# Recurrence of a delta-rule attention block: column sums moved to TensorE, two matrices in turns on VectorE, GpSimd left out

## The chip, the cores and the metric

The kernel runs on one core of one Trainium2 chip. The metric is the time of one execution of the whole program on the device, in microseconds (us). Before the change three runs gave a median of 5632.02 us (5631.69 to 5635.43).

## The reference, cut to what matters

The program is two transformer layers in float32 on an input of 2 x 2048 tokens with 128 features. The changed part is the first sublayer of layer 0, a chunked attention with a matrix memory M (8 x 8 for each of 16 heads) that every token updates:

```python
k = k / jnp.maximum(jnp.linalg.norm(k, axis=-1, keepdims=True), 1e-12)
alpha = jax.nn.sigmoid(alpha_raw) * 0.5
beta = jax.nn.sigmoid(beta_raw) * 2.0
def t_step(M, kv):
    k_t, v_t = kv
    Mk = jnp.einsum('bhde,bhe->bhd', M, k_t)
    forget = Mk[..., :, None] * k_t[..., None, :]
    write = v_t[..., :, None] * k_t[..., None, :]
    return (M - alpha * forget + beta * write, None)
```

M is updated token by token over 64-token chunks, each chunk reads M as it stood at its start, and the rest of the sublayer is a softmax attention inside the chunk. The kernel cuts the 4096 tokens into 128 pieces of 32 tokens, one to a partition. The effect of a piece on M is an affine map: M becomes M A + B. So a recurrence of 32 steps, run for all 128 pieces at once, works out A (the decay rows, starting from the identity) and B (the write rows, starting from zero) for every head. A later, short scan puts the 128 maps together.

## The kernel before, in words

`two_layer_kernel` runs its stages one after another; an all-engine barrier stands between them. The change lies in the first of the three blocks of `delta_attention_stage`, which the lines below number as the profile does.

**Ahead of the recurrence.** SyncE (SP) loads inputs. VectorE (DVE) normalises the input groups; TensorE (PE) transposes them (L243) into `hT`, ScalarE (ACT) copies them out of PSUM (L268), and PE makes q, k, v of each of the 32 positions with one matmul each (L250), which ACT copies to `qs`, `ks`, `vs` (L271 to L273). `hT` isn't read again in this stage. DVE normalises `ks` (L323 to L329), multiplies `vs` by beta in 32 instructions (L337), sets `state` to zero and its decay rows to the identity (L339, L340), and lets GpSimd (POOL) go.

**The recurrence.** `state` is [128 pieces, 16 heads, 16 rows, 8 columns]: rows 0 to 7 of a head are A, rows 8 to 15 are B. A step multiplies the state by the key (L347), sums over the 8 columns (L348), multiplies by alpha, which carries its minus sign (L349), adds the value to the write rows (L350), multiplies that vector by the key (L351) and adds the product to the state (L352). DVE does this for heads 0 to 11 in a hardware loop of 32 turns; each instruction waits for the one before it. POOL does the same for heads 12 to 15 in a loop of its own (L290 to L300), with the key copied first and the column sums made by three halving additions (L294 to L296). The two engines don't wait for each other inside the loops. PE and ACT have nothing to do.

**Behind it.** DVE waits for POOL (L354), lays the state out anew in two copies (L355, L356) and releases PE (L357), which makes 16 transposes in four groups (L258); ACT copies each group out (L277). That ends the block. The next block is the scan over the 128 pieces (L376 on POOL, L388 on PE, L413 on DVE), then come the chunk attention and all other stages, none of which the change touches. SP stores q, k and v to DRAM in the same block (L228 to L235) and isn't waited for inside it, but for the DVE's wait for the first two stores ahead of L337.

`Steps` gives each instruction of an engine a semaphore increment and, unless `settle=False`, makes the engine wait for it. `wait(eng, sem, value)` is a wait that falls away for values of zero and below.

Of the kernel before, what the change touches and what calls it, by code (L numbers as in the profile page):

```python
# [13 lines left out]
ALU = mybir.AluOpType  # L14
AX = mybir.AxisListType
# [41 lines left out]
def wait(eng, sem, value):  # L57

    if not isinstance(value, int) or value > 0:
        eng.wait_ge(sem, value)  # L60
# [103 lines left out]
def delta_attention_stage(nc, x_dram, xr, mods, w_qkvT, w_oT, alpha_raw, beta_raw, tables, qkv_dram):  # L164

    H, DH, SUB, N_SUB = 16, 8, 32, 128
    with ExitStack() as ctx:
        sem = ctx.enter_context(stage_semaphores(nc, "da"))
        keep = lambda n, shape, dt=F32: ctx.enter_context(nc.sbuf_tensor(f"da_{n}", shape, dt))  # L170
        mem = keep("mem", [128, 64, 128])
        ident = keep("ident", [128, 128])
# [5 lines left out]
        with ExitStack() as c2:  # L178
            sb = lambda n, shape, dt=F32: c2.enter_context(nc.sbuf_tensor(f"da_{n}", shape, dt))
            ps = [c2.enter_context(nc.psum_tensor(f"da_psa{i}", [128, 512], F32)) for i in range(8)]  # L180
            hT = sb("hT", [128, 4096])
            st, mv = sb("st", [128, 4, 6]), sb("mv", [128, 4, 2])
            mean, var, rstd, half, tmp = (sb(n, [128, 32]) for n in ("mean", "var", "rstd", "half", "tmp"))
            h = sb("h", [128, 2, 4, 128])
# [4 lines left out]
            state = sb("state", [128, H, 16, DH])  # L189
            prod = sb("prod", [128, H, 16, DH])  # L190
            dots = sb("dots", [128, H, 16])

            flat_state = prod[:, :, :, :].rearrange("p a b c -> p a (b c)")
# [6 lines left out]
            state_init, pool_state_done, pool_seq, ones_set = sem("state_init"), sem("pool_state_done"), sem("pool_seq"), sem("ones_set")  # L200

            H_DVE = 12
            key = sb("key", [128, DH * (H - H_DVE)])

            def recurrence_operands(t, hs):

                k_t = ks[:, ds(t, 1), :].rearrange("p o (h e) -> p (o h) e", e=DH)[:, hs, :]
                v_t = vs[:, ds(t, 1), hs, 0:DH].rearrange("p o h e -> p (o h) e")
                n = hs.stop - hs.start
                kb = k_t.rearrange("p h (o e) -> p h o e", o=1).to_broadcast([128, n, 16, DH])  # L210
                ub = dots[:, hs, :].rearrange("p h (r o) -> p h r o", o=1).to_broadcast([128, n, 16, DH])
                return kb, ub, v_t, alpha[:, hs].rearrange("p (h o) -> p h o", o=1).to_broadcast([128, n, 16])

            with nc.Block() as block:
# [22 lines left out]
                def _(pe):  # L237
# [13 lines left out]

                    pe.wait_ge(state_done, 1)
                    pe.wait_ge(v_out, SUB)
                    for j in range(4):
                        wait(pe, tr_done, 2 * (j - 1))
                        for i in range(4):
                            n = 4 * j + i
                            last = nc.tensor.transpose(ps[j % 2][:, 128 * i:128 * i + 128], flat_state[:, n, :], ident[:, :])  # L258
                        last.then_inc(tr_ps, 1)
# [19 lines left out]
                @block.gpsimd  # L279
                def _(pool):  # L280
                    step = Steps(pool, pool_seq)

                    nc.gpsimd.memset(vs[:, :, :, DH:DH + 1], 1.0).then_inc(ones_set, 1)
                    pool.wait_ge(state_init, 1)
                    hs = slice(H_DVE, H)
                    with pool.Fori(0, SUB) as t:
                        step.turn(0, t, 9)
                        _, ub, v_t, alpha_b = recurrence_operands(t, hs)
                        k_t = ks[:, ds(t, 1), DH * H_DVE:DH * H].rearrange("p o d -> p (o d)")
                        step(nc.gpsimd.tensor_copy(key[:, :], k_t))  # L290
                        kb = key[:, :].rearrange("p (h o e) -> p h o e", o=1, e=DH).to_broadcast([128, H - H_DVE, 16, DH])
                        step(nc.gpsimd.tensor_tensor(prod[:, hs, :, :], state[:, hs, :, :], kb, ALU.mult))

                        step(nc.gpsimd.tensor_tensor(prod[:, hs, :, 0:4], prod[:, hs, :, 0:4], prod[:, hs, :, 4:8], ALU.add))  # L294
                        step(nc.gpsimd.tensor_tensor(prod[:, hs, :, 0:2], prod[:, hs, :, 0:2], prod[:, hs, :, 2:4], ALU.add))
                        step(nc.gpsimd.tensor_tensor(dots[:, hs, :], prod[:, hs, :, 0], prod[:, hs, :, 1], ALU.add))  # L296
                        step(nc.gpsimd.tensor_tensor(dots[:, hs, :], dots[:, hs, :], alpha_b, ALU.mult))
                        step(nc.gpsimd.tensor_tensor(dots[:, hs, DH:16], dots[:, hs, DH:16], v_t, ALU.add))
                        step(nc.gpsimd.tensor_tensor(prod[:, hs, :, :], ub, kb, ALU.mult))
                        step(nc.gpsimd.tensor_tensor(state[:, hs, :, :], state[:, hs, :, :], prod[:, hs, :, :], ALU.add))  # L300
                    pool.sem_inc(pool_state_done, 1)

                @block.vector
                def _(dve):
# [14 lines left out]
                    flat = prod[:, :, :, :].rearrange("p a b c -> p (a b c)")  # L319
# [14 lines left out]
                    for t in range(0, SUB, 8):  # L334
                        for i in range(8):
                            vi = vs[:, t + i, :, 0:DH]
                            step(nc.vector.tensor_tensor(vi, vi, beta[:, :].rearrange("p (h o) -> p h o", o=1).to_broadcast([128, H, DH]), ALU.mult), settle=(i == 7))  # L337

                    step(nc.vector.memset(state[:, :, :, :], 0.0))  # L339
                    step(nc.vector.memset(state[:, :, :, :].rearrange("p h r e -> p h (r e)")[:, :, 0:64:9], 1.0))  # L340
                    dve.sem_inc(state_init, 1)
                    before = step.base + step.n
                    hs = slice(0, H_DVE)
                    with dve.Fori(0, SUB) as t:
                        step.turn(before, t, 6)
                        kb, ub, v_t, alpha_b = recurrence_operands(t, hs)
                        step(nc.vector.tensor_tensor(prod[:, hs, :, :], state[:, hs, :, :], kb, ALU.mult))  # L347
                        step(nc.vector.tensor_reduce(dots[:, hs, :], prod[:, hs, :, :], AX.X, ALU.add))  # L348
                        step(nc.vector.tensor_tensor(dots[:, hs, :], dots[:, hs, :], alpha_b, ALU.mult))  # L349
                        step(nc.vector.tensor_tensor(dots[:, hs, DH:16], dots[:, hs, DH:16], v_t, ALU.add))  # L350
                        step(nc.vector.tensor_tensor(prod[:, hs, :, :], ub, kb, ALU.mult))  # L351
                        step(nc.vector.tensor_tensor(state[:, hs, :, :], state[:, hs, :, :], prod[:, hs, :, :], ALU.add))  # L352
                    step.turn(before, SUB, 6)
                    dve.wait_ge(pool_state_done, 1)  # L354
                    step(nc.vector.tensor_copy(flat_state[:, 0:DH, :].rearrange("p e (h r) -> p h r e", r=DH), state[:, :, 0:DH, :]))  # L355
                    step(nc.vector.tensor_copy(flat_state[:, DH:16, :].rearrange("p d (h e) -> p h d e", e=DH), state[:, :, DH:16, :]))  # L356
# [1868 lines left out]
```

## Time and profile before

| what | value |
|---|---|
| median of 3 runs | 5632.02 us |
| time of the profiled execution | 5640.35 us |
| span of its trace, first to last instruction | 5638.6 us |
| granted TensorE clock, mean | 0.901 |
| busy: PE, DVE, ACT, POOL | 82%, 72%, 56%, 53% |
| the recurrence (L347 to L357) | about 142 to 493 us of the span |

### The profile page before, as it was taken

Reading aid. Unit: us, or ns where it says so; the run is one execution under the profiler, and the core shown is the slowest. Engines: PE = TensorE matmul, PEld = TensorE weight load, DVE = VectorE, ACT = ScalarE, POOL = GpSimd, SP = SyncE. Lnnn points to the kernel's source line nnn. Section 1 sums busy time; section 2 is a strip of 40 time slices with the busy share of each in tenths; the row PEclk is TensorE's granted clock in tenths of the full one; section 3 lists DMA queues with packets and bytes.
Section 4 is the critical chain, followed back from the end, with each engine's and each line's share of the span. In section 5 each row is a group of like instructions: output and inputs, shape, how many; then the busy total and the mean of one; then the engine's idle time right before and its main releaser. Section 6 shows DMA issues by size and latency. Waiting matters only on the chain. (4 is left out here: it accounts for less than half of the span.)

```text
span 5638.6 us, 215664 instructions
## 1 busy us (share of the span) xinstructions
PE 4650.3 (82%) x78080; PEld 3324.1 (59%) x78080; DVE 4062.7 (72%) x8694; ACT 3158.8 (56%) x6668; POOL 2979.6 (53%) x4109
## 2 busy tenths in 40 slices
PE   2004776999999999999999999999992874998997
PEld 2003653666666666667666767676762553666665
DVE  5995557777777777777777777777775446776675
ACT  1000443677677767766676767676761122676675
POOL 0887104666666666666666666666650001555552
PEclk6555887999999999999999999999996567999998
DMA  1000114454545454545454555554540002443342
GB/s 69 0 0 0 35 31 118 123 140 128 138 127 138 126 141 128 138 131 138 131 134 131 136 134 131 135 133 134 131 119 15 0 0 61 114 112 109 107 113 77
DMA packets 708750, 564.88 MB, mean 100 GB/s; under 512 B 227460, under 2 KB 633704, under 8 KB 707848
## 3 DMA queue, kind: packets, MB, share of 16 engines
q1 hardware_dynamic: 694920, 538.05, 36.3%
q10 hardware_dynamic: 13312, 22.02, 1.2%
q14 instruction: 449, 3.68, 0.2%
q8 instruction: 69, 1.13, 0.1%
HBM read 360.07 MB, written 200.02 MB: 99 GB/s over the span
## 5 line engine op out<-in xcount | busy, mean ns | idle before, releaser
L2080 POOL TENSOR_TENSOR L_qk<-L_cos_part,L_sin_part 128x512 f32<-128x512 f32 x896 | 1128.9, 1274 | 165.0 <-DVE L_sin_part L1965 164.6
L1750 ACT ACTIVATE L_squares<-L_ps_q 128x512 f32<-128x512 f32 x896 | 535.0, 597 | 981.1 <-PE L_ps_q L1502 975.0
L1502 PE MATMUL L_ps_q<-L_w_qkv,L_xT 128*128 128x512 f32 x1792 | 971.8, 625 | 27.8 <-DVE L_sin_part L1965 10.2
L2071 POOL TENSOR_TENSOR L_qk<-L_qk,L_rnorm 128x1024 f32<-128x1024 f32 (+1 forms) x512 | 864.7, 1689 | 20.3 <-POOL L_rnorm L2061 0.5
L1537 PEld LDWEIGHTS L_ps_t<-L_ident,L_qk 128*128 128x128 f32 x3584 | 446.4, 141 | 474.6 <-issue 376.4
L1964 DVE TENSOR_TENSOR L_cos_part<-L_ps_q,L_rot 128x512 f32<-128x512 f32 x896 | 610.3, 681 | 43.0 <-POOL L_rot L2090 35.1
L1965 DVE TENSOR_TENSOR L_sin_part<-L_ps_q,L_rot 128x512 f32<-128x512 f32 x896 | 610.1, 681 | 0.0
L1966 DVE TENSOR_REDUCE L_sumsq<-L_squares 128x8 f32<-128x512 f32 x896 | 605.7, 676 | 0.0
L2055 POOL TENSOR_TENSOR L_nw_a<-L_rnorm 128x32 f32<-128x32 f32 (+1 forms) x256 | 60.0, 234 | 1026.6 <-ACT L_rnorm L1780 1026.5
L1537 PE MATMUL L_ps_t<-L_ident,L_qk 128*128 128x128 f32 x3584 | 539.4, 273 | 2.5 <-POOL L_qk L2071 1.9
L1761 ACT ACTIVATE L_qkT<-L_ps_t 128x512 f32<-128x512 f32 x896 | 530.0, 591 | 13.9 <-PE L_ps_t L1537 13.5
L1589 PEld LDWEIGHTS L_ps_t<-L_ident,L_probs 128*128 128x128 f32 x2048 | 215.2, 141 | 413.7 <-issue 350.1
L2090 POOL TENSOR_TENSOR L_rot<-L_rot_base,L_qk_scales 128x256 f32<-128x256 f32 x256 | 187.3, 732 | 506.6 <-DMA L_qk_scales<-in_L_ffn_k_scale 500.3
L1603 PE MATMUL L_ps_q<-L_w_out,L_outT 128*128 128x128 f32 x3584 | 445.8, 276 | 2.8 <-ACT L_outT L1769 1.7
L1603 PEld LDWEIGHTS L_ps_q<-L_w_out,L_outT 128*128 128x128 f32 x3584 | 422.1, 193 | 5.1 <-issue 4.4
L1634 PE MATMUL L_ps_s<-L_qkT 64*32 64x64 f32 (+1 forms) x26624 | 415.1, 228 | 0.2 <-ACT L_qkT L1761 0.2
L1930 DVE RECIPROCAL L_p_rec<-L_ps_o 128x8 f32<-128x8 f32 (+1 forms) x512 | 103.0, 201 | 408.2 <-PE L_ps_o L1655 302.6
L1574 PE MATMUL L_ps_t<-L_w_qkv,L_xT 128*128 128x512 f32 x768 | 393.7, 594 | 0.6 <-issue 0.6
L1949 DVE TENSOR_TENSOR L_probs<-L_ps_s,L_neg_max 128x512 f32<-128x512 f32 x512 | 354.4, 692 | 53.2
L1589 PE MATMUL L_ps_t<-L_ident,L_probs 128*128 128x128 f32 x2048 | 327.5, 283 | 75.1 <-issue 62.8
L1634 PEld LDWEIGHTS L_ps_s<-L_qkT 64*32 64x32 f32 (+1 forms) x26624 | 322.0, 107 | 108.2 <-issue 108.2
L1935 DVE TENSOR_TENSOR L_att<-L_ps_o,L_p_rec 128x512 f32<-128x512 f32 (+1 forms) x512 | 320.2, 625 | 53.2
(295 smaller groups left out, 9429.7 us busy)
## 6 DMA issues: line engine op xcount, KB each, us to landing
L_val<-v_rows SPq DMA_DIRECT2D x896, 260.0 KB, 3.9
v_rows<-L_val SPq DMA_DIRECT2D x384, 260.0 KB, 2.1
v_rows<-L_val SPq DMA_DIRECT2D x512, 65.0 KB, 2.0
L_rot_base<-in_rot SPq DMA_DIRECT2D x256, 128.0 KB, 2.1
v_rows<-L_val SPq DMA_DIRECT2D x128, 130.0 KB, 2.1
L_x_in<-x_rows SPq DMA_DIRECT2D x512, 32.0 KB, 1.7
mid_rows<-z SPq DMA_DIRECT2D x256, 64.0 KB, 1.6
L_f_in<-mid_rows SPq DMA_DIRECT2D x256, 64.0 KB, 2.0
```

What stands on the lines that cost most here:

```text
L1502: nc.tensor.matmul(ps_q[j % 2][:, :], xT[:, parity(t), :], w_qkv[:, 0:2, 256 * j:256 * j + 256], start=True, stop=True).then_inc(S["proj_p ...
L1537: last = nc.tensor.transpose(ps_t[0][:, 128 * i:128 * i + 128], qk[:, parity(t), h, s, 128 * i:128 * i + 128], ident[:, :])
L1589: last = nc.tensor.transpose(ps_t[2 - NS][:, 128 * i:128 * i + 128], probs[:, h, 128 * i:128 * i + 128], ident[:, :])
L1603: last = nc.tensor.matmul(ps_q[0][:, 0:128], outT[:, u, :], w_out[:, u, :], start=(u == 0), stop=(u == U - 1))
L1634: last = nc.tensor.matmul(S_VIEW[W * a:W * a + W, p, i, :], qkT[rows, 0, u, W + W * a:2 * W + W * a], qkT[rows, kk, u, W * a:W * a + 2 * W ...
L1750: nc.scalar.activation(squares[:, j % 2, :], ps_q[j % 2][:, :], ACT.Square).then_inc(S["sq_done"], 1)
L1761: nc.scalar.activation(dst, ps_t[0][:, :].rearrange("x (a u q) -> x a u q", a=2, u=2), ACT.Copy).then_inc(S["qkT_done"], 1)
L1964: nc.vector.tensor_tensor(R4(cos_part[:, j % 2, :]), qkp, cs[:, :, 0, :, :, :].to_broadcast([128, 2, 4, 2, 32]), ALU.mult)
L1965: nc.vector.tensor_tensor(R4(sin_part[:, j % 2, :]), qkp[:, :, :, ::-1, :], cs[:, :, 1, :, :, :].to_broadcast([128, 2, 4, 2, 32]), ALU.mul ...
L1966: nc.vector.tensor_reduce(sumsq[:, t % 2, j, :], squares[:, j % 2, :].rearrange("x (g d) -> x g d", g=8), AX.X, ALU.add).then_inc(S["ss_do ...
L2071: nc.gpsimd.tensor_tensor(v, v, r, ALU.mult).then_inc(S["normed"], 1)
L2080: nc.gpsimd.tensor_tensor(qk[:, t % 2, h, s, :], cos_part[:, j % 2, :], sin_part[:, j % 2, :], ALU.add).then_inc(S["added"], 1)
```

## The change

`state` and `prod` become [128, 2, 8, 128]: part 0 is A (decay), part 1 is B (write); within a part the column comes first, then head and row. Each part has 1024 elements in a partition, all on DVE.

A step for one part is now: DVE multiplies the part by the key times alpha (`k_forget`, made once beforehand for all steps, in the memory of `hT`); PE adds the eight columns of the product with eight matmuls against the identity into one PSUM bank (and for part 1 adds the value, times beta, with a ninth); DVE multiplies that sum, read from PSUM, by the key; DVE adds the product to the part. DVE takes the two parts in turns. Both loops, DVE's and PE's, are written out over the 32 steps. POOL's loop is gone; POOL only writes the ones column of `vs`, as before. The products with beta and with alpha are one instruction each. The identity is set by eight small memsets. At the end one copy lays part 1 out anew; part 0 is transposed as it stands.

```diff
-            state = sb("state", [128, H, 16, DH])
-            prod = sb("prod", [128, H, 16, DH])
-            dots = sb("dots", [128, H, 16])
+            state = sb("state", [128, 2, DH, 128])
+            prod = sb("prod", [128, 2, DH, 128])
...
+            k_forget = hT[:, :].rearrange("p (t d) -> p t d", t=SUB)
+            def over_rows(k):
+                return k.rearrange("p (h e o) -> p e h o", e=DH, o=1).to_broadcast([128, DH, H, DH])
+            def blocks(a):
+                return a.rearrange("p e (h r) -> p e h r", r=DH)
...
                 # TensorE
+                    for t in range(SUB):
+                        for part in range(2):
+                            pe.wait_ge(multiplied[part], t + 1)
+                            for e in range(DH):
+                                last = nc.tensor.matmul(ps[2 + part][:, 0:128], ident[:, :], prod[:, part, e, :], start=(e == 0), stop=(part == 0 and e == DH - 1))
+                            if part == 1:
+                                last = nc.tensor.matmul(ps[3][:, 0:128].rearrange("p (h d) -> p h d", d=DH), ident[:, :], vs[:, t, :, 0:DH], start=False, stop=True)
+                            last.then_inc(summed[part], 1)
...
-                            last = nc.tensor.transpose(ps[j % 2][:, 128 * i:128 * i + 128], flat_state[:, n, :], ident[:, :])
+                            last = nc.tensor.transpose(ps[j % 2][:, 128 * i:128 * i + 128], (state[:, 0, n, :] if n < DH else prod[:, 1, n - DH, :]), ident[:, :])
                 # GpSimd: the whole loop of L287 to L301 goes
...
                 # VectorE
-                    for t in range(0, SUB, 8):
-                        for i in range(8):
-                            vi = vs[:, t + i, :, 0:DH]
-                            step(nc.vector.tensor_tensor(vi, vi, beta[:, :].rearrange("p (h o) -> p h o", o=1).to_broadcast([128, H, DH]), ALU.mult), settle=(i == 7))
+                    vb = vs[:, :, :, 0:DH]
+                    per_head = lambda a: a[:, :].rearrange("p (o h u) -> p o h u", o=1, u=1).to_broadcast([128, SUB, H, DH])
+                    nc.vector.tensor_tensor(vb, vb, per_head(beta), ALU.mult).then_inc(factors, 1)
+                    nc.vector.tensor_tensor(k_forget.rearrange("p t (h e) -> p t h e", e=DH), ks[:, :, :].rearrange("p t (h e) -> p t h e", e=DH), per_head(alpha), ALU.mult).then_inc(factors, 1)
                     step(nc.vector.memset(state[:, :, :, :], 0.0))
...
+                    for e in range(DH):
+                        nc.vector.memset(blocks(state[:, 0, :, :])[:, e, :, e], 1.0).then_inc(state_init, 1)
+                    dve.wait_ge(state_init, DH)
+                    dve.wait_ge(factors, 2)
+                    def multiply(part, t):
+                        wait(dve, updated[part], t)
+                        nc.vector.tensor_tensor(blocks(prod[:, part, :, :]), blocks(state[:, part, :, :]), over_rows(k_forget[:, t, :]), ALU.mult).then_inc(multiplied[part], 1)
+                    def update(part, t):
+                        dve.wait_ge(summed[part], t + 1)
+                        u = ps[2 + part][:, 0:128].rearrange("p (o h r) -> p o h r", o=1, r=DH).to_broadcast([128, DH, H, DH])
+                        nc.vector.tensor_tensor(blocks(prod[:, part, :, :]), u, over_rows(ks[:, t, :]), ALU.mult).then_inc(outer[part], 1)
+                        dve.wait_ge(outer[part], t + 1)
+                        nc.vector.tensor_tensor(state[:, part, :, :], state[:, part, :, :], prod[:, part, :, :], ALU.add).then_inc(updated[part], 1)
+                    multiply(0, 0)
+                    for t in range(SUB):
+                        multiply(1, t)
+                        update(0, t)
+                        if t + 1 < SUB:
+                            multiply(0, t + 1)
+                        update(1, t)
+                    for part in range(2):
+                        dve.wait_ge(updated[part], SUB)
+                    step(nc.vector.tensor_copy(prod[:, 1, :, :].rearrange("p d (h e) -> p e h d", e=DH), blocks(state[:, 1, :, :])))
                     dve.sem_inc(state_done, 1)
```

## Rows read from the trace of the kernel before

**Rows 1.** The chain of waits from 132 to 500 us: who waited, us in total, times, longest

```profile
PE da_psa L258 <- DVEq L357: 383.5, 1, 383.5
...
DVE da_prod L347 <- DVE da_state L352: 13.1, 31, 0.5
...
DVE da_prod L355 <- POOLq L301: 6.6, 1, 6.6
```

**Rows 2.** Busy time by stretch: length, PE, PEld, DVE, ACT, POOL, clock, DMA

```profile
142.00:491.00 349.00, 0.00 (x0) 0.00 (x0) 320.52 (x192) 0.00 (x0) 312.53 (x288) 0.50 0.00 0
```

**Rows 3.** Timeline of one late recurrence step: start us, duration us, engine, line, operation

```profile
463.33 2.60 DVE L347 TENSOR_TENSOR da_prod<-da_state,da_ks 128x1536 f32<-128x1536 f32 x1 [0.42 <-DVE da_state L352]
...
465.97 1.75 DVE L348 TENSOR_REDUCE da_dots<-da_prod 128x192 f32<-128x1536 f32 x1
...
469.53 2.65 POOL L300 TENSOR_TENSOR da_state<-da_state,da_prod 128x512 f32<-128x512 f32 x1
471.10 2.70 DVE L352 TENSOR_TENSOR da_state<-da_state,da_prod 128x1536 f32<-128x1536 f32 x1
...
474.22 2.60 DVE L347 TENSOR_TENSOR da_prod<-da_state,da_ks 128x1536 f32<-128x1536 f32 x1 [0.42 <-DVE da_state L352]
```

**Rows 4.** Timeline of DVE around the recurrence's start, 126 to 152 us

```profile
127.65 4.43 DVE L329 TENSOR_TENSOR da_ks<-da_ks,da_rk 128x4096 f32<-128x4096 f32 x1
132.11 6.93 DVE L337 TENSOR_TENSOR da_vs<-da_vs,da_beta 128x128 f32<-128x128 f32 x32
139.53 1.76 DVE L339 MEMSET da_state<- 128x2048 f32 x1 [0.49 <-DVE da_vs L337]
141.49 0.17 DVE L340 MEMSET da_state<- 128x128 f32 x1 [0.19 <-DVE da_state L339]
142.01 1.79 DVE L347 TENSOR_TENSOR da_prod<-da_state,da_ks 128x1536 f32<-128x1536 f32 x1 [0.36 <-DVE da_state L340]
143.84 1.75 DVE L348 TENSOR_REDUCE da_dots<-da_prod 128x192 f32<-128x1536 f32 x1
```

**Rows 5.** Timeline of DVE at 1942 us: PSUM inputs, no wait for the instruction before

```profile
1941.62 0.68 DVE L1964 TENSOR_TENSOR L_cos_part<-L_ps_q,L_rot 128x512 f32<-128x512 f32 x1
1942.21 0.68 DVE L1965 TENSOR_TENSOR L_sin_part<-L_ps_q,L_rot 128x512 f32<-128x512 f32 x1
```

**Rows 6.** Timeline of DVE at 67 us: L103 waits for L102 just before it

```profile
67.79 0.69 DVE L102 TENSOR_TENSOR da_h<-da_h,mods 128x512 f32<-128x512 f32 x1
68.52 0.69 DVE L103 TENSOR_TENSOR da_h<-da_h,mods 128x512 f32<-128x512 f32 x1
```

**Rows 7.** Timeline of PE: the group of transposes released by that L103

```profile
69.27 1.12 PE L243 MATMUL da_psa<-da_ident,da_h 128*128 128x128 f32 x4 [1.30 <-DVE da_h L103]
```

**Rows 8.** Timeline of PEld, one record for each half of a 384-column matmul

```profile
88.04 0.34 PEld L250 LDWEIGHTS da_psa<-da_w,da_hT 128*128 128x128 f32 x1 [0.30 <-issue]
88.68 0.34 PEld L250 LDWEIGHTS da_psa<-da_w,da_hT 128*128 128x128 f32 x1 [0.30 <-issue]
```

**Rows 9.** Timeline of PE at 937 us: eight 128-column float32 matmuls

```profile
937.64 1.95 PE L1603 MATMUL L_ps_q<-L_w_out,L_outT 128*128 128x128 f32 x16
```

**Rows 10.** Busy time of PE by stretch: length, busy (records), granted clock, DMA

```profile
66.00:85.00 19.00, 8.63 (x32) 0.50 0.00 0
86.00:92.00 6.00, 6.00 (x10) 0.50 0.00 0
92.00:109.00 17.00, 17.00 (x54) 1.00 0.01 1
...
580.00:590.00 10.00, 7.00 (x43) 0.99 0.01 2
590.00:600.00 10.00, 4.74 (x21) 0.52 0.19 51
600.00:610.00 10.00, 7.05 (x224) 0.97 0.24 59
```

**Rows 11.** Timeline around the recurrence's end: DVE, PE, ACT

```profile
491.26 1.26 DVE L355 COPY da_prod<-da_state 128x1024 f32<-128x1024 f32 x1 [6.59 <-POOLq L301]
492.56 0.69 DVE L356 COPY da_prod<-da_state 128x1024 f32<-128x1024 f32 x1
...
493.36 3.84 PE L258 MATMUL da_psa<-da_ident,da_prod 128*128 128x128 f32 x16 [383.52 <-DVEq L357]
494.58 0.60 ACT L277 ACTIVATE da_trans_a<-da_psa 128x512 f32<-128x512 f32 x1 [384.09 <-PE da_psa L258]
...
497.30 0.60 ACT L277 ACTIVATE da_trans_b<-da_psa 128x512 f32<-128x512 f32 x1 [0.26 <-PE da_psa L258]
```

**Rows 12.** Timeline of PE at 957 us: a train that stops with nothing to wait for

```profile
957.29 0.39 PE L1655 MATMUL L_ps_o<-L_val,L_probsT 64*32 64x65 f32 x18 [1.48 <-issue]
```

More of the change, by code:

```diff
@@ L188, in delta_attention_stage @@
             vs = sb("vs", [128, SUB, H, DH + 1])
-            state = sb("state", [128, H, 16, DH])
-            prod = sb("prod", [128, H, 16, DH])
-            dots = sb("dots", [128, H, 16])
-            flat_state = prod[:, :, :, :].rearrange("p a b c -> p a (b c)")
+            state = sb("state", [128, 2, DH, 128])
+            prod = sb("prod", [128, 2, DH, 128])
             rk, rk_half, rk_tmp, rk_x = (sb(n, [128, SUB * H]) for n in ("rk", "rk_half", "rk_tmp", "rk_x"))
@@ L198, in delta_attention_stage @@
             k_normed, stored, state_done, tr_ps, tr_done = (sem(n) for n in ("k_normed", "stored", "state_done", "tr_ps", "tr_done"))
[L200 to L212, printed above, removed]
+            ones_set = sem("ones_set")
+            state_init, factors = sem("state_init"), sem("factors")
+            multiplied, summed, outer, updated = ([sem(f"{n}_{part}") for part in ("decay", "write")] for n in ("multiplied", "summed", "outer", "updated"))
+            k_forget = hT[:, :].rearrange("p (t d) -> p t d", t=SUB)
[3 more added lines that the diff above has]
+                return a.rearrange("p e (h r) -> p e h r", r=DH)
             with nc.Block() as block:
@@ L280, in _ @@
                 def _(pool):
-                    step = Steps(pool, pool_seq)
                     nc.gpsimd.memset(vs[:, :, :, DH:DH + 1], 1.0).then_inc(ones_set, 1)
[L284 to L301, printed above, removed]
                 @block.vector
@@ L318, in _ @@
                     dve.wait_ge(k_out, SUB)
-                    flat = prod[:, :, :, :].rearrange("p a b c -> p (a b c)")
+                    flat = prod[:, :, :, :].rearrange("p a e x -> p (a e x)")
                     kf = ks[:, :, :].rearrange("p t d -> p (t d)")
@@ L339, in _ @@
+                    nc.vector.tensor_tensor(vb, vb, per_head(beta), ALU.mult).then_inc(factors, 1)
+                    nc.vector.tensor_tensor(k_forget.rearrange("p t (h e) -> p t h e", e=DH), ks[:, :, :].rearrange("p t (h e) -> p t h e", e=DH), per_head(alpha), ALU.mult).then_inc(factors, 1)
                     step(nc.vector.memset(state[:, :, :, :], 0.0))
-                    step(nc.vector.memset(state[:, :, :, :].rearrange("p h r e -> p h (r e)")[:, :, 0:64:9], 1.0))
-                    dve.sem_inc(state_init, 1)
@@ L342, in _ @@
[L342 to L356, printed above, removed]
+                    for e in range(DH):
+                        nc.vector.memset(blocks(state[:, 0, :, :])[:, e, :, e], 1.0).then_inc(state_init, 1)
```

## The prediction

> **What bounds the kernel now.** I began with the granted clock and the waits. The chain that ended last shows only the final stage, so I took the waits of the stretch of the change: PE sits 383.5 us for DVE's release behind the recurrence, and nothing else waits there for long [rows 1]. Stages stand between barriers, so every microsecond by which that release comes earlier shortens the program. The busy times by stretch say who works: of 349 us DVE is busy 320.5, POOL 312.5, PE and ACT not at all, with the clock at half [rows 2]. Neither loop waits for the other by a semaphore, yet both are slow. The timeline shows how: a turn takes 10.89 us (463.33 to 474.22), and in it the same 1536-element instruction that took 1.79 us in the first turn takes 2.60, and the state's addition 2.70 [rows 3, 4]. The instruction that runs with one SBUF input, the sum over columns, takes 1.75 both times. So the bound is DVE and POOL together: their instructions hold each other up. POOL ends last, by 6.6 us [rows 1].
>
> **The change part by part.** *Cost of a DVE instruction.* New ones have 1024 elements. Durations at 512, 1536 and 4096 elements are 0.69, 1.76 to 1.79 and 4.43 us [rows 4, 6]; they lie on a line of 1.042 us per 1000 elements plus 0.16, which gives 1.23 us at 1024. A PSUM input doesn't make it dearer: 0.68 at 512 [rows 5]. Start to start it depends on the wait: an instruction that waits for the one before follows after 0.73 us at 512 (0.533 us of elements and 0.19), one that doesn't after 0.59 to 0.60 (0.533 and 0.065) [rows 5, 6]. At 1024 these are 1.26 and 1.13 us.
>
> *DVE's step.* Six instructions for each t. The first product waits for the part's addition just before it, the addition waits for the outer product just before it: four pitches of 1.26. Each outer product follows a product that it doesn't depend on: two of 1.13. Together 7.30 us, and 32 x 7.30 = 233.6 us. With POOL idle I take the undisturbed durations. POOL's nine instructions a turn, alpha's and the value's additions (L349, L350) and the loop's 0.42 us [rows 3] are gone.
>
> *PE's step.* 17 matmuls of 128 columns, 34 records. At 2.4 GHz sixteen records take 1.95 us, their last one's tail included, some 0.112 each [rows 9]. At 1.2 GHz a record of 384 columns takes 0.64 us start to start, so 0.213 for 128 [rows 8]. Handing over costs 0.06 us from DVE to PE (68.52 + 0.69 to 69.27 [rows 6, 7]) and 0.1 from PE's end (493.36 + 1.12) to the reader [rows 7, 11]. Eight sums are then ready 0.06 + 1.95 + 0.1 = 2.1 us after the product at full clock, nine after 2.3; at half clock 0.06 + 16 x 0.213 + 0.2 of tail + 0.1 = 3.8 and 4.2. Between a product's end and the moment DVE wants its sum lie the other part's outer product and addition and one more product: 1.13 - 0.10 + 2 x 1.26 = 3.55 us. So at full clock PE hides with 1.2 us to spare. Without that cover, at half clock, 0.2 and 0.65 us of each step show: 8.15 us a step.
>
> *Start.* At the first sum there is only one product to hide behind (3.8 - 1.1 = 2.6 us at half clock), and I give a step or so to the clock's rise: 3.6 us. Recurrence: 237.2.
>
> *Ahead of it.* The 32 small instructions (6.93 us) go; two of 4096 elements come at 4.43 each, the second overlapped: 8.8. The memset stays at 1.76, and eight tiny ones take the place of one; each costs between 0.07 and 0.17 (L340 [rows 4]), I take 0.8 in all. The loop's entry (0.36 [rows 4]) goes. From 132.11 the first product starts at about 143.8 instead of 142.0: 1.8 lost. SP's three stores run beside this and nobody new waits for them; POOL's and SP's queues get nothing.
>
> *Behind it.* The last addition ends at 143.8 + 237.2 = 381.0. One copy with a strided output stays, at L355's 1.26, not L356's 0.69 [rows 11], and 0.2 for its waits; PE's transposes start at 382.6 against 493.36: 110.8 won. PE comes to them warm: four take some 0.7 instead of 1.12, and ACT's four copies become the bound; about 1.1 won of the 4.5 from 493.36 to the last copy's end [rows 11]. The scan behind begins with POOL, so a warm PE wins it nothing that I count.
>
> **Sum.** 5640.35 (the profiled execution; its span is 5638.6) - 111.9 = 5528.4. The median is 8.3 us below that execution, so the prediction for the median is 5632.0 - 111.9 = **5520**.
>
> **A page against the rows.** The pitch depends on the semaphore wait: 0.73 us with one on the instruction before, 0.60 without [rows 5, 6]. The Trainium skill (VectorE: DVE Perf Modes, The DRAIN you can't avoid) says that the next instruction starts only when the pipe is empty and that "the semaphore costs nothing extra here". The trace doesn't agree; by that rule all six pitches would be alike.
>
> **The rivals.**
> *All pitches alike.* If waits cost nothing, a step is 6 x 1.13 = 6.8 us and the time 5504; if there is never an overlap, 6 x 1.26 = 7.56 and 5528. Rows 5 and 6 speak against both, though neither pair has this kernel's operands. The first is the page's rule above. 0.04 and 0.08; the second stays within my range.
>
> *The clock stays or falls back to 1.2 GHz.* PE would then need 7.25 us of 8.15 a step. For: PE busy in bursts for 8.63 of 19 us left it at half, and it fell after a stretch with 4.74 of 10 busy. Against: six us of uninterrupted matmuls raised it, and it stayed up with 7.0 of 10 busy [rows 10]. Here records fill (2.0 + 2.2) / 7.3 = 0.57 of the time at full clock, between those two, but 0.9 at half clock, so it is raised whenever it falls. At half clock throughout: 32 x 8.15 = 261, time 5546; alternating, between. The Trainium skill (TensorE: Matmul & The Clock Gate, A second HAM failure mode: psum-queue depth-cycling) tells of a kernel that cycled PSUM banks with short idles and saw the clock oscillate; no row here shows that for this pattern. 0.12.
>
> *Weight loads aren't hidden (slower).* Each record brings a load of the identity. At half clock such a load is recorded with 0.34 us [rows 8], more than the 0.213 that the columns take. If loads ran in series with 128-column records, the step would be at least 34 x 0.34 = 11.6 us, 32 x 11.6 = 370, and the time 5520 + (370 - 237) = 5653, slower. It decides from a record pitch of about 0.31 us on, where a step reaches (237.2 + 111.9) / 32 = 10.9 us, what it is today. Against: at full clock sixteen records with their loads take 1.95 us [rows 9], and four transposes at half clock 1.12 [rows 7], so loads overlap. 0.02.
>
> *Instruction supply.* 1088 matmuls and some 190 DVE instructions are written out, no loop. A train of PE stopped once for 1.48 us with nothing to wait for [rows 12]. On PE 1.2 us of each is hidden; on DVE none is. A dozen stops on both would cost 5 to 15 us. 0.06.
>
> *It does nothing.* That POOL isn't what slows DVE, and 1024 elements cost as much as in rows 3 (1.45 times): step 10.6, time about 5626. Rows 4 exclude it nearly. 0.01.
>
> **How the numbers follow.** The forecast case has 0.67 and gives 5520 with 5 us to either side for setup, handovers and shifted later stages. The range reaches from there over part of the first rival to the cold clock and a few supply stops: 5510 to 5550. No change can be told from noise within 0.2% (11 us). Faster takes all cases but the serial loads and part of the last: 0.97, same 0.01, slower 0.02.
>
> **What would show it.** The six DVE instructions at 1.22 to 1.23 us, none near 1.7; pitches 1.26, 1.13, 1.26 in turn; a step of 7.3; the wait of DVE for PE near zero but at the first sum; PE's records 0.112 apart and the clock at 1.0 from some 10 us into the recurrence; PE released at about 383 us; the scan behind unchanged in length. I am wrong if DVE waits for PE each step, if the clock stands at 0.5 there, if pitches are alike, or if stages behind the block change by more than 3 us.

## The result, and the profile after

The changed kernel takes 5504.03 us (median of four runs, 5502.36 to 5505.12) against 5633.73 us for the kernel before on the same chip: a ratio of 0.9771 with a 95% interval of 0.9759 to 0.9783, 129.7 us less. The forecast was 5520 with a range of 5510 to 5550. The sign and the mechanism were right; the time came out 6 us below the range. One rival of the prediction has this very time, 5504 for pitches that are all alike; the pitches below speak against it. One run of the kernel before, beside e9 to e11, was slow at 8020.41 us, and the ratios leave it out.

The span is 5502.0 us, and the profiled execution took 5503.74. From the page, busy times with counts, then the granted clock in 40 slices:

```profile
PE 4777.1 (87%) x79168; PEld 3443.6 (63%) x79168; DVE 3958.7 (72%) x8670; ACT 3156.6 (57%) x6668; POOL 2667.5 (48%) x3821
...
PEclk6987979999999999999999999999995567999998
```

PE has 1088 records more, the 34 a step of the 32 steps. To see where time went, I took each stage's length from its first to its last instruction. The block with the recurrence shrank from 461.9 us (36.0 to 497.9) to 349.0 (34.7 to 383.7): 112.9 us, where the prediction's sum has 111.9. So the missing part isn't in the recurrence. The rest of the program, whose code is the same, became shorter by 136.6 - 112.9 = 23.7 us in the two profiled executions, and by 129.7 - 112.9 = 16.8 if the medians are taken: the profiled execution of before lies 7 us above its median.

The recurrence in the timeline of the kernel after, one full step (start us, duration us, engine, line, operation):

```profile
150.28 1.22 DVE L341 TENSOR_TENSOR da_prod<-da_psa,da_ks 128x1024 f32<-128x1024 f32 x1
...
150.42 2.05 PE L254 MATMUL da_psa<-da_prod,da_ident 128*128 128x128 f32 x16 [1.32 <-DVE da_prod L335]
151.53 1.23 DVE L343 TENSOR_TENSOR da_state<-da_state,da_prod 128x1024 f32<-128x1024 f32 x1
152.79 1.22 DVE L335 TENSOR_TENSOR da_prod<-da_state,da_hT 128x1024 f32<-128x1024 f32 x1
153.94 1.22 DVE L341 TENSOR_TENSOR da_prod<-da_psa,da_ks 128x1024 f32<-128x1024 f32 x1
...
155.18 1.23 DVE L343 TENSOR_TENSOR da_state<-da_state,da_prod 128x1024 f32<-128x1024 f32 x1
...
156.44 1.23 DVE L335 TENSOR_TENSOR da_prod<-da_state,da_hT 128x1024 f32<-128x1024 f32 x1
157.59 1.22 DVE L341 TENSOR_TENSOR da_prod<-da_psa,da_ks 128x1024 f32<-128x1024 f32 x1
```

Read the start times: 150.28, 151.53, 152.79, 153.94, 155.18, 156.44, 157.59. The pitches are 1.25, 1.26 and 1.15 in turn and a step is 7.31 us; [rows 3] had 10.89. An outer product, which waits for nothing that DVE has just done, starts 0.07 us before the product ahead of it ends. Sixteen records of PE take 2.05 us and lie wholly beside DVE.

The chain of waits from 142 to 380 us has for DVE one line, the first sum:

```profile
DVE da_prod L341 <- PE da_psa L254: 2.7, 1, 2.7
```

The busy time of PE by stretch in the kernel after (length, busy by records, granted clock, DMA) shows the rise and fall of the clock, and the timeline the end of the block:

```profile
142.00:147.50 5.50, 4.70 (x22) 0.50 0.00 0
147.50:160.00 12.50, 7.98 (x64) 1.00 0.01 1
376.00:379.60 3.60, 0.23 (x2) 1.00 0.00 0
379.60:383.00 3.40, 3.40 (x16) 0.50 0.00 0
```

```profile
378.17 1.09 DVE L354 COPY da_prod<-da_state 128x1024 f32<-128x1024 f32 x1
...
379.37 1.78 PE L265 MATMUL da_psa<-da_ident,da_state 128*128 128x128 f32 x8 [3.83 <-DVEq L355]
...
383.11 0.60 ACT L284 ACTIVATE da_trans_b<-da_psa 128x512 f32<-128x512 f32 x1 [0.26 <-PE da_psa L265]
```

The clock is at 2.4 GHz from 147.5 us on, 5 us after the first sum began, and the whole recurrence keeps it (PE is busy for 0.60 of the time from 143 to 371 us by its records). After 3.8 us without a matmul it is at 1.2 GHz again from 379.6 us on, just behind the transposes' start, so they take from 379.37 to 383.71, 4.3 us, against 4.5 before [rows 11].

### The profile page after: what moved, and what is told of

Its sections match the earlier page's. It is cut to its first block and busy times, and to the rows that moved or that the text cites. A ratio compares the mean times of both kernels' runs of the same rounds, so it can differ in the third digit from the quotient of the medians.

```text
span 5502.0 us, 216728 instructions
## 1 busy us (share of the span) xinstructions
PE 4777.1 (87%) x79168; PEld 3443.6 (63%) x79168; DVE 3958.7 (72%) x8670; ACT 3156.6 (57%) x6668; POOL 2667.5 (48%) x3821
## 3 DMA queue, kind: packets, MB, share of 16 engines
q8 instruction: 77, 1.26, 0.1%
## 5 line engine op out<-in xcount | busy, mean ns | idle before, releaser
L1500 PE MATMUL L_ps_q<-L_w_qkv,L_xT 128*128 128x512 f32 x1792 | 969.4, 623 | 23.7 <-DVE L_sin_part L1963 11.0
```

What stands on the lines that cost most here:

```text
L1500: nc.tensor.matmul(ps_q[j % 2][:, :], xT[:, parity(t), :], w_qkv[:, 0:2, 256 * j:256 * j + 256], start=True, stop=True).then_inc(S["proj_p ...
```

## The experiments

Medians of before stand beside each experiment's own, from the same chip. "Block" is the length of the stage with the recurrence, "first" and "second" are the two local-block stages behind it; all three from the profiled execution, one for each kernel.

| kernel | block | first | second | median |
|---|---|---|---|---|
| before | 461.9 | 3402.9 | 881.1 | 5633.7 |
| after | 349.0 | 3389.8 | 874.4 | 5504.0 |
| e3 before, no POOL loop | 377.9 | 3401.3 | 881.2 | 5554.1 |
| e7 before, all heads on DVE | 450.6 | 3401.2 | 881.2 | 5625.2 |
| e8 after, POOL busy | 436.4 | 3389.9 | 874.3 | 5592.2 |
| e4 after, no turns | 600.1 | 3392.5 | 873.1 | 5758.2 |
| e1 before, PE code | 461.4 | 3398.0 | 881.2 | 5629.1 |
| e2 after, PE shift | 349.1 | 3396.9 | 873.8 | 5510.5 |
| e5 before, DVE code | 461.2 | 3396.8 | 877.3 | 5623.6 |
| e6 after, 64 on DVE | 349.0 | 3413.8 | 873.8 | 5530.1 |
| e11 after, 128 on DVE | 349.1 | 3390.7 | 869.9 | 5505.5 |
| e12 before, both codes | 461.8 | 3398.6 | 874.5 | 5625.4 |
| e9 trim | 342.8 | 3397.0 | 873.9 | 5507.3 |
| e10 trim, warm | 342.1 | 3389.9 | 873.0 | 5502.4 |

**Is it contention? e3: POOL's loop taken out of the kernel before, and heads 12 to 15 with it.**

```diff
-                    pool.wait_ge(state_init, 1)
...
-                        step(nc.gpsimd.tensor_tensor(state[:, hs, :, :], state[:, hs, :, :], prod[:, hs, :, :], ALU.add))
```

> The kernel before without POOL's loop: heads 12 to 15 are left out, VectorE's 12 heads stay. Theory (VectorE and POOL hold each other up): VectorE's 1536-element products fall from 2.5 to 1.76 us, a step from 10.9 to 8.5, the block by 77 + 6.6 us, the time to about 5550. Rival (the instructions are slow for their operands, and POOL only ends late): a step stays above 10 us and only the 6.6 us of waiting go, 5627.

Measured: 5554.06 us against 5633.59, a ratio of 0.986 (0.9845 to 0.9876); the block 377.9 us, 84.0 less. Its timeline:

```profile
198.62 1.76 DVE L330 TENSOR_TENSOR da_prod<-da_state,da_ks 128x1536 f32<-128x1536 f32 x1 [0.42 <-DVE da_state L335]
...
204.79 1.76 DVE L335 TENSOR_TENSOR da_state<-da_state,da_prod 128x1536 f32<-128x1536 f32 x1
206.97 1.76 DVE L330 TENSOR_TENSOR da_prod<-da_state,da_ks 128x1536 f32<-128x1536 f32 x1 [0.42 <-DVE da_state L335]
```

The products and the addition fell to 1.76 us from the 2.60 and 2.70 of [rows 3] and a turn to 8.35. The two loops did hold each other up, with no semaphore between them.

**What is that worth by itself? e7: all 16 heads on DVE, as before otherwise.**

```diff
-                    hs = slice(0, H_DVE)
+                    hs = slice(0, H)
```

(and POOL's loop out, as in e3)

> The recurrence as before, but all 16 heads on VectorE and none on POOL: no PE sums, no contention. A step of 12 heads took 8.35 us with POOL's loop taken out; 512 more elements in four instructions (2.13) and a tenth for the small ones make 10.6, so the block is about 449 us and the time 5625. That would show that leaving POOL idle by itself is worth some 10 us, and that PE's sums are worth the other 100. Rival (POOL alone is the trouble and VectorE has room): a step below 9 us and a time near 5560.

Measured: 5625.17 us against 5633.51, ratio 0.9984 (0.9975 to 0.9994); the block 450.6 us, the 2048-element instructions 2.29 us each. So POOL's quarter of the work had cost DVE more than it saved: with all heads on DVE the block is 11 us shorter. The other 101.6 us of the change's 112.9 are the rest of the change. What they consist of can be read from e7's timeline:

```profile
199.26 2.29 DVE L334 TENSOR_TENSOR da_prod<-da_dots,da_ks 128x2048 f32<-128x2048 f32 x1
...
206.62 2.29 DVE L331 TENSOR_REDUCE da_dots<-da_prod 128x256 f32<-128x2048 f32 x1
208.94 0.42 DVE L332 TENSOR_TENSOR da_dots<-da_dots,da_alpha 128x256 f32<-128x256 f32 x1
209.51 0.29 DVE L333 TENSOR_TENSOR da_dots<-da_dots,da_vs 128x128 f32<-128x128 f32 x1
209.84 2.29 DVE L334 TENSOR_TENSOR da_prod<-da_dots,da_ks 128x2048 f32<-128x2048 f32 x1
```

A step takes 10.58 us. The column sum and the two small instructions, which the change takes off DVE, have 3.22 us of it (206.62 to 209.84), 103 us in 32 steps. The other 7.36 us, three instructions of 2048 elements and the loop's turn, are about what the six of 1024 elements take in the kernel after (7.31).

**The same contention, made in the new kernel. e8: POOL at work beside it.**

```diff
+                    pool.wait_ge(factors, 2)
+                    with pool.Fori(0, 150) as t:
+                        step.turn(1, t, 1)
+                        step(nc.gpsimd.tensor_tensor(junk[:, 0, :], junk[:, 1, :], junk[:, 2, :], ALU.mult))
```

> The changed kernel with POOL multiplying 512-element tiles of its own in SBUF 150 times beside the recurrence. Theory (instructions of VectorE with two SBUF inputs and instructions of POOL exclude each other): L335 and L343 rise from 1.22 to between 1.8 and 2.5 us, the outer product L341, which has one input in PSUM, keeps 1.22, the step rises from 7.3 to 10 or more while POOL works, the time to 5560 to 5600. Rival (only POOL's work on the same tiles did harm): a step of 7.3 and a time of 5504.

Measured: 5592.18 us against 5633.51 (0.9929, 0.9914 to 0.9944), 88 us above the changed kernel; the block takes 436.4 us, 87.4 more. From its timeline, a stretch of the recurrence and the end of the block:

```profile
198.80 1.22 DVE L351 TENSOR_TENSOR da_state<-da_state,da_prod 128x1024 f32<-128x1024 f32 x1
199.21 1.93 POOL L296 TENSOR_TENSOR da_junk<-da_junk 128x512 f32<-128x512 f32 x1 [0.45 <-POOL da_junk L296]
...
200.06 2.17 DVE L343 TENSOR_TENSOR da_prod<-da_state,da_hT 128x1024 f32<-128x1024 f32 x1
...
202.16 1.21 DVE L349 TENSOR_TENSOR da_prod<-da_psa,da_ks 128x1024 f32<-128x1024 f32 x1
...
209.27 2.17 DVE L343 TENSOR_TENSOR da_prod<-da_state,da_hT 128x1024 f32<-128x1024 f32 x1
...
443.14 0.60 ACT L286 ACTIVATE da_trans_b<-da_psa 128x512 f32<-128x512 f32 x1 [0.26 <-PE da_psa L267]
...
469.65 1.26 POOL L296 TENSOR_TENSOR da_junk<-da_junk 128x512 f32<-128x512 f32 x1 [0.45 <-POOL da_junk L296]
```

Not all of the 88 us are contention. A step takes 9.2 us (200.06 to 209.27) instead of 7.31, less than the 10 that I expected, and 32 of them make 60 us. The block's work is done at 443.74; then the barrier waits 27 us for the rest of POOL's 150 instructions, which take 1.26 us each when DVE is idle.

POOL's instruction starts during the addition (L351), is recorded with 1.93 us and ends at 201.14; the product (L343), begun meanwhile, is recorded with 2.17 and ends 1.09 us after POOL's, little less than its usual time. The tiles have nothing in common, so it isn't the data. My expectation was half right: I had the addition slower too, but it keeps 1.22 to 1.23 us in all 64 records. POOL is the one that is late there, since the two engines fall into step. The outer product, which has one input in PSUM, keeps 1.21. The Trainium skill (SBUF — State Buffer, SBUF: two separate sides) calls the port pair that VectorE and GpSimd share an exclusive lock, which a VectorE instruction with two SBUF inputs needs and the loser waits for; the trace agrees with both halves of it, 2.17 us with two SBUF inputs and 1.21 with one.

**Does the cover matter? e4: the parts one after another.**

```diff
-                        multiply(1, t)
-                        update(0, t)
...
+                        for part in range(2):
+                            multiply(part, t)
+                            update(part, t)
```

> The changed kernel with the parts one after another on VectorE (product, sum, outer product, addition of one part, then of the other), so that nothing covers PE's sums. If the clock stays at 2.4 GHz a step is 1.23 + 2.1 + 1.26 + 1.13 and the same with 2.3, 11.7 us, and the time 5504 + 32 x 4.4 = 5644. If it falls to 1.2 GHz, the sums take 3.8 and 4.2 us, a step is 15.2 and the time about 5757. PE would be busy for 0.36 of the time at full clock, which I expect to be too little to hold it: above 5700.

Measured: 5758.18 us against 5633.59, ratio 1.0221 (1.0205 to 1.0236), slower than before the change. The first fence is its timeline, the second its busy time of PE by stretch:

```profile
303.19 3.78 PE L254 MATMUL da_psa<-da_prod,da_ident 128*128 128x128 f32 x16 [3.71 <-DVE da_prod L335]
...
307.44 1.22 DVE L341 TENSOR_TENSOR da_prod<-da_psa,da_ks 128x1024 f32<-128x1024 f32 x1 [4.30 <-PE da_psa L256]
```

```profile
300.00:620.00 320.00, 164.19 (x714) 0.62 0.00 0
```

The same 16 records take 3.78 us instead of 2.05, and DVE waits 4.30 us for nine sums: the prices that the prediction put on half clock, 3.8 and 4.2. The clock isn't at half all the time here, its mean is 0.62, yet a step takes 15.2 us as if it were. The turns buy two things, the cover and the clock. By the estimate in the expectation, at 2.4 GHz throughout the serial order would have come to 5644: then the cover is worth 140 us and the clock the other 114. No run has the one without the other.

**Where do the 17 us outside the block come from? e1, e2, e5, e6, e11, e12.** All other stages have the same code, but it lies elsewhere, since the written-out steps stand ahead of it. How long the recurrence takes isn't what moves them. In e3 the block is 84 us shorter than before and in e7 11 us, and the two local-block stages have 3401 and 881 us in both, against 3403 and 881; in e4 and e8 it is 251 and 87 us longer than in the changed kernel, and they have 3392.5 and 873.1, 3389.9 and 874.3.

e1, to the kernel before:

```diff
+                    for n in range(544):
+                        nc.tensor.matmul(ps[6][:, 0:128], ident[:, :], ident[:, :], start=True, stop=True)
                     pe.wait_ge(state_done, 1)
```

> The kernel before with 544 more float32 matmuls of the identity on PE, into a PSUM bank that nobody reads, ahead of the wait for the recurrence's end; they run beside the recurrence. Theory (the 17 us that the change won outside its own block come from where PE's later code lies, since these matmuls shift it as the changed kernel's do): the recurrence keeps its 10.9 us a step and the block its 462 us, the local-block stages get 8 to 20 us shorter, and the time is 5614 to 5626. Rival (they come from something else in the change, such as the clock or the other engines' code): the stages behind keep their lengths within 2 us, and the time is 5633 within 3.

Measured: 5629.11 against 5633.59, ratio 0.9991 (0.9982 to 1.0000): 4.5 us, less than the theory had and with an interval that reaches no change at all, and the second stage didn't move. PE's code alone isn't it.

e2, the same for 16 matmuls ahead of the sums of the kernel after:

> The changed kernel with 16 more identity matmuls (64 PE instructions) ahead of its sums, hidden beside VectorE's normalisation. Theory (code place): nothing changes in the block, but the local-block stages change by 3 to 15 us in either direction, because the same loops now begin elsewhere. Rival: the time is 5504 within 3.

Measured: 5510.48 against 5633.59 (0.9774, 0.9761 to 0.9787). The block is the same, the first local stage 7 us longer. Its five runs go from 5497.9 to 5515.1, so the median alone would say little, and the stage lengths are those of the slowest of the five.

e5, to the kernel before, and e6 with 64 instead of 192, to the kernel after:

```diff
+                    for n in range(192):
+                        nc.vector.memset(spare[:, n:n + 1], 0.0)
                     dve.wait_ge(k_out, SUB)
```

> The kernel before with 192 one-column memsets on VectorE, in the 25 us in which it waits for the keys anyway; they stand for the DVE instructions that the change writes out. Theory (the last stages' gain comes from where VectorE's later code lies): the two long stops of VectorE in the second local-block stage (5.0 us ahead of L1930, once in each loop turn) shrink to about 2.6, that stage falls from 881 to 873 to 876 us, and the time to about 5622 to 5628. Rival: the stage stays at 881 and the time at 5633.

Measured: 5623.62 against 5633.51, ratio 0.9982 (0.9973 to 0.9991). The long stops shrank as expected, from 9.8 us in two to 5.4, though the stage, at 877.3, kept 3 us of its difference. More came from the first stage, 3402.9 to 3396.8, which I had not expected, so the total is right in part by luck. The stops are these, in the chain of waits of e5 and in the timelines of the kernels before and after; "issue" means that DVE waited for nothing that the profile shows:

```profile
DVE L_p_rec L1933 <- issue: 5.4, 2, 2.7
```

```profile
5116.68 0.18 DVE L1930 RECIPROCAL L_p_rec<-L_ps_o 128x4 f32<-128x4 f32 x1 [5.03 <-issue]
```

```profile
4984.40 0.18 DVE L1928 RECIPROCAL L_p_rec<-L_ps_o 128x4 f32<-128x4 f32 x1 [2.64 <-issue]
```

The line is the first of the loop's next turn. In the kernel before the clock falls to 1.2 GHz at it for 6.8 us (3.4 in the second of the two turns), which makes 2.4 us of lateness into 3.8 in the first. PE by stretch in the kernel before:

```profile
5116.50:5123.20 6.70, 5.66 (x17) 0.50 0.27 72
```

> The changed kernel with 64 one-column memsets on VectorE in the same wait. Theory (code place): the block keeps 349 us, the second local-block stage leaves 874 us for up to 881 or stays, depending on where the loops fall, and the time lies between 5497 and 5515. Rival (the gain behind the block has another cause): 5504 within 2 and both stages as in the changed kernel.

Measured: 5530.11 against 5633.51, ratio 0.9815 (0.98 to 0.983): 26 us lost to 64 instructions of 0.07 us in a stretch in which DVE waits anyway. That is beyond the 5515 that I had allowed. The block kept 349.0 and the second stage 873.8; the first grew by 24 us, some 2 in each of its loop turns of 278 us. The chain of waits of that stage, this kernel first, then the kernel after:

```profile
DVE L_p_rec L1931 <- issue: 35.1, 10, 3.7
```

```profile
DVE L_p_rec L1928 <- issue: 26.6, 10, 2.9
```

The ten stops, one in each turn, account for 8.5 of the 24 us. In nine turns the clock then falls to 1.2 GHz for some 3.4 us, which costs about 1 us more each; in the kernel after it stays at 2.4 GHz from 782 to 4120 us. PE by stretch behind the same stop, this kernel first:

```profile
1842.10:1845.40 3.30, 3.30 (x8) 0.50 0.09 21
```

```profile
1830.30:1833.60 3.30, 3.27 (x16) 1.00 0.10 22
```

Stops and clock together are some 17 us; where the other 7 go stays open.

e11, 128 memsets in the same place:

> The changed kernel with 128 one-column memsets on VectorE instead of the 64 that cost 26 us. The profile's instruction queue moves packets of 8192 bytes. If code is loaded in blocks of 128 instructions and only its place within a block counts, 128 more are no shift at all: 5504 within 3. If any added code costs, or the place counts on a larger scale, it stays at or above 5530, or lands elsewhere.

Measured: 5505.46 against 5633.07 (0.9775, 0.9758 to 0.9793), the first stage 3390.7:

```profile
DVE L_p_rec L1931 <- issue: 26.5, 10, 2.9
```

Twice as many instructions, and that stage's loss is gone. An instruction queue's packet has some 8200 bytes (440 packets, 3.60 MB on the page of the kernel after). That one loop got back its old time after a shift of 128 fits loading by blocks of 128 instructions, if an instruction takes a 128th of a packet, which no run here shows. One shift of 64 and one of 128 are all that was tried, so the block size is an inference. And 128 isn't no shift for every stage: in this execution the scan behind the block took 95.0 us against 91.1 in the kernel after, and the second stage 869.9 against 874.4. The two nearly cancel, so that the total is back at 5505 is in part luck.

e12, e1 and 151 memsets together in the kernel before, the change's net number of instructions on both engines:

> The kernel before with 544 matmuls on PE as in e1 and 151 one-column memsets on VectorE: the net numbers of instructions that the change adds on the two engines. Theory (the 17 us outside the block are code place on PE and VectorE alone): the block keeps 462 us, the two local-block stages take 3388 to 3393 and 873 to 875 us as in the changed kernel, and the time is 5614 to 5620. Rival (something of the changed recurrence carries over into later stages): 5626 or more.

Measured: 5625.36 against 5635.16, ratio 0.998 (0.9971 to 0.9989), 9.8 us. The second stage is that of the changed kernel, 874.5, and so are its stops, 5.1 us in two (the kernel before has 9.8 in two):

```profile
DVE L_p_rec L1935 <- issue: 5.1, 2, 2.6
```

The first isn't: 3398.6. Eleven turns of its loop still have PE late by 0.36 us behind one group of transposes; here in e12, then at the same place in the kernel after:

```profile
1679.47 0.60 PE L1542 MATMUL L_ps_t<-L_ident,L_qk 128*128 128x128 f32 x4
1680.33 0.63 PE L1561 MATMUL L_ps_t<-L_ident,L_att 128*128 128x128 f32 x4 [0.25 <-DVE L_att L1940]
```

```profile
1561.22 0.60 PE L1535 MATMUL L_ps_t<-L_ident,L_qk 128*128 128x128 f32 x4
1561.71 0.63 PE L1554 MATMUL L_ps_t<-L_ident,L_att 128*128 128x128 f32 x4
```

That is 4 us. e5, which has memsets alone, doesn't have it. PE's waits at that line in the first stage, for the kernel before, the kernel after, e12 and e5:

```profile
PE L_ps_t L1556 <- DVE L_att L1935: 21.1, 28, 1.9
```

```profile
PE L_ps_t L1554 <- DVE L_att L1933: 18.8, 17, 1.9
```

```profile
PE L_ps_t L1561 <- DVE L_att L1940: 22.2, 28, 1.9
```

```profile
PE L_ps_t L1559 <- DVE L_att L1938: 18.4, 17, 2.2
```

e5 loses its time elsewhere: at DVE's first stop of that stage it is 7 us behind the kernel after (522.9 against 515.5 us from the stage's start), and at the tenth still 7 (3019.0 against 3012.2).

So of 17 us about ten (6 to 16 by e12's interval) are shown to be the place of DVE's and PE's code, because a kernel with the old recurrence wins them by padding alone. The time lies between the theory's 5620 and the rival's 5626, so for the rest the rival isn't excluded. Of the other seven, 4 are the late turns, which e5's padding removes and e12's doesn't, so they depend on the place as well; 3 stay open. No padding won it all at once.

**Can it be better? e9 and e10.** e9 takes the first step out of the loop (its sums are known) and puts the identity's memsets into the wait for the keys:

```diff
+                    nc.vector.tensor_tensor(blocks(prod[:, 0, :, :]), first_u, over_rows(ks[:, 0, :]), ALU.mult).then_inc(outer[0], 1)
+                    nc.vector.tensor_tensor(blocks(state[:, 1, :, :]), vs[:, 0:1, :, 0:DH].to_broadcast([128, DH, H, DH]), over_rows(ks[:, 0, :]), ALU.mult).then_inc(updated[1], 1)
...
-                    for t in range(SUB):
+                    for t in range(1, SUB):
```

> The changed kernel with its first step taken out of the loop (the decay rows are the identity and the write rows zero there, so both sums are known: the key times alpha, and the value), the identity's memsets moved into VectorE's wait for the keys. By the rows: 2.4 us of memsets, and 3.9 us of the first step (its two products, one addition and a sum), so the block falls from 349 to about 342.7. The whole time depends on where the later code comes to lie, which moved it by up to 26 us in the run before: 5498 if it lies as well, up to 5523 if not. If code place were no cause, 5498 within 2.

Measured: 5507.31 against 5633.07 (0.9775, 0.9758 to 0.9793). The block takes 342.8, as worked out to 0.1 us, and the first local stage takes 7 us more. What was won in the block was lost behind it.

> As e9_trim, with 17 matmuls of the identity on PE just ahead of the first sum and three tiny memsets on VectorE, so that PE and DVE have as many instructions ahead of the later stages as in the changed kernel. Two expectations: the clock is at 2.4 GHz at the first sum, whose wait falls from 2.7 to about 1.0 us, so the block takes 341; and with the code where it lay, the stages behind take what they take in the changed kernel (3390 and 874), so the time is 5504 - 8 = 5496. Rival: place of code isn't counted in instructions alone, and the stages behind differ by more than 3 us.

Measured: 5502.41 against 5633.07 (0.9772, 0.9754 to 0.9789). With the counts restored the first local stage is back at 3389.9, and the second at 873.0. The block is 342.1, not 341: the 17 matmuls did raise the clock, but PE then stood idle for 3.7 us, the clock was back at half 0.7 us into the sums, and the first sum's wait fell only from 2.7 to 2.17.

```profile
141.00:144.50 3.50, 0.00 (x0) 1.00 0.00 0
144.50:149.00 4.50, 4.41 (x24) 0.62 0.00 0
```

The scan behind took 95.0 us instead of 91.1 in this execution, as it did in e11 (92.8 in e9); why stays open, and it takes back more than half of what the block won. At 5502.4 (5499.95 to 5509.31), where I expected 5496, it can't be told from the changed kernel; the 7 us that the block is shorter are real, and the whole doesn't show them.

## Why the prediction missed

*Durations and pitches.* Right: 1.22 to 1.23 us each; pitches 1.25, 1.26 and 1.15 against 1.26, 1.26 and 1.13; a step 7.31 against 7.30. The rule of the Trainium skill (VectorE: DVE Perf Modes, The DRAIN you can't avoid) that a semaphore costs nothing extra would make the pitches alike. With 1.26 behind a wait for the instruction before and 1.15 without one, the trace disagrees with it here as it did before. The same section says as well that a next instruction that isn't held starts earlier, and with that the trace agrees: the 1.15.

*PE's cover and the clock.* Right: 2.05 us at full clock for 16 records (1.95 predicted), hidden, and 3.78 at half clock (e4). The clock rose some 6 us into the recurrence and stayed.

*Start, setup and end.* The wait at the first sum was 2.7 (2.6). DVE's setup took 11.3 us from L323 to the first product (11.7), the copy 1.09 (1.26). Wrong was the 1.1 us for warm transposes: PE has nothing to do for 3.8 us between the last sum and the transposes, the clock is at half for them, and 0.2 came.

*Sum of the block.* 112.9 measured, 111.9 predicted. That it is so close is partly luck: the transposes began 112.7 us earlier in the block, not 110.8, because the work ahead of them was shorter than each of its terms (0.4 us for the setup, 0.7 for the recurrence, some 0.3 for the copy and its waits, 0.6 ahead of L323, which the prediction didn't cost), and the 0.9 us that the transposes fell short took half of that back.

*What failed* is the last step, "5 us to either side for setup, handovers and shifted later stages". Later stages were costed at nothing. They gained 16.8 us by the medians, outside that allowance; the block's miss is 1.0 us and the new median of the kernel before lies 1.7 higher, and 5520.1 - 1.0 - 16.8 + 1.7 is 5504.0. The prediction's own sign of being wrong, that stages behind the block change by more than 3 us, came true: the first local-block stage became 13.1 us shorter and the second 6.7. In its place the runs showed that the same loops run at another speed when code ahead of them is added or removed; padding alone won 9.8 us in e12. The rows had a hint that I read only one way: the PE train that stops "with nothing to wait for" [rows 12] became a rival about the new code's own supply. It should have been turned around as well. Loops elsewhere stop for the same reason, and writing out 32 steps moves all of them; e6 shows 26 us for one such move, so the range needed some 15 to 25 us on both sides of the forecast, the lower side too. The rival of supply stops in the new code didn't occur: DVE has one wait in the whole recurrence.

## What to carry to other kernels

If a helper engine runs the same kind of element work out of SBUF beside VectorE, compare one instruction's duration with and without it: here GpSimd's quarter of the heads made VectorE's instructions with two SBUF inputs 1.45 to 1.53 times as long (2.60 and 2.70 us), and the block was 11 us shorter without it. Give TensorE the sums, but only with a second, independent chain to cover them, since the serial order lost both the cover and the clock and ended 2% slower than the start. And when a change adds or removes instructions ahead of long loops, read its gain from the length of its own stage: in this kernel the same loops moved the total by up to 26 us for where they came to lie.

## What was not expected of the hardware

- Sixty-four memsets of 0.07 us each, in a stretch where VectorE waits anyway, cost 26 us, and 128 left the total where it was (5530.1 and 5505.5), though two stages moved by some 4 us each, one up and one down.
- A lateness of 2.4 us of VectorE at a loop's turn let TensorE's clock fall for 6.8 us, so that 3.8 us were lost.
- Two loops that contend fall into step: in e8 the addition never waited for GpSimd (1.23 us), and the product always did (2.17 us in nearly all records).
